# Edge softmax of a graph layer: 20 one-hot columns in four groups of five, 44 gathered columns, instead of 18 in three groups of six and 46 gathered

## The reference, cut to what matters

```
h = (x_flat @ W_gat).reshape(M, HEADS, NUM_EXPERTS)      # M = 16384 nodes, 4 x 4 values each
a_src = (h * att_src).sum(-1)
e = leaky_relu(a_src[src] + a_dst[dst], negative_slope=0.2)
e_max = segment_max(e, dst, num_segments=M)
ee = exp(e - e_max[dst])
denom = segment_sum(ee, dst, num_segments=M)
msg = h[src] * (ee / (denom[dst] + 1e-16))[:, :, None]
agg = segment_sum(msg, dst, num_segments=M)
```

## Time and profile before

| | |
|---|---|
| median of 3 runs | 7383.86 us (7380.45 to 7390.46) |
| the profiled execution | 7389.08 us, of which the span of its instructions is 7387.4 us |
| busy, share of the span | PE 76%, DVE 70%, ACT 37%, POOL 33% |
| the edge stage | from GpSimd's first gather at 3383.8 to about 5574 us |
| gathers in it (L2702) | 1472, busy 1718.7 us |
| matmuls of the columns (L2720) | 6912 |

### The profile page before, as it was taken

How to read it: one execution, slowest core, us unless ns; L and a number is a source line. 1 busy time by engine, 2 the same in 40 slices (tenths; PEclk the granted TensorE clock), 3 DMA queues, 4 the chain that set the end, 5 groups by cost and what they waited for, 6 DMA issues and landing times. The chain is left out here.

```text
span 7387.4 us, 113310 instructions
## 1 busy us (share of the span) xinstructions
PE 5582.5 (76%) x43709; PEld 2955.6 (40%) x43709; DVE 5138.4 (70%) x9355; ACT 2731.1 (37%) x4639; POOL 2413.2 (33%) x2214
## 2 busy tenths in 40 slices
PE   4759799868479999725978777877840579769998
PEld 3642266522146666522434333333420148623332
DVE  7869987877978888714866666666642466667776
ACT  3534433343256666512423223322310242323332
POOL 0000000000068400047777777777775210000000
PEclk8869899979779999957988889888975789879999
DMA  0000000012021000000111110110110000000001
GB/s 15 1 5 6 20 15 26 3 33 63 24 36 19 10 2 2 7 35 7 26 17 21 23 21 17 22 21 17 23 22 12 5 2 3 2 15 1 1 1 23
DMA packets 129314, 115.00 MB, mean 16 GB/s; under 512 B 72354, under 2 KB 113475, under 8 KB 127107
## 3 DMA queue, kind: packets, MB, share of 16 engines
q1 hardware_dynamic: 65278, 85.60, 3.9%
q0 software_dynamic: 63616, 23.35, 3.0%
q10 hardware_dynamic: 12, 0.39, 0.0%
HBM read 36.72 MB, written 37.86 MB: 10 GB/s over the span
## 5 line engine op out<-in xcount | busy, mean ns | idle before, releaser
L2702 POOL DMA_INDIRECT X<-gat_node_table,edges_idx x1472 | 1718.7, 1168 | 454.1 <-issue 454.1
L2720 PE MATMUL edges_bank<-XT,edges_hotT 128*128 128x512 bf16 x4608 | 1408.2, 388 | 0.0
L2720 PE MATMUL edges_bank<-X,edges_hotT 128*128 128x512 bf16 x2304 | 896.0, 389 | 388.3 <-ACT edges_hotT L2746 388.3
L2753 ACT COPY XT<-edges_bank 128x512 f32<-128x512 f32 x576 | 337.2, 585 | 993.1 <-PE edges_bank L2720 993.1
L2720 PEld LDWEIGHTS edges_bank<-XT,edges_hotT 128*128 128x128 bf16 x4608 | 459.1, 100 | 502.8 <-issue 47.4
L2720 PEld LDWEIGHTS edges_bank<-X,edges_hotT 128*128 128x128 bf16 x2304 | 229.7, 100 | 608.7 <-issue 413.7
L2821 DVE TENSOR_TENSOR XT<-XT,edges_mask 128x3072 f32<-128x3072 f32 x96 | 322.6, 3361 | 214.7 <-ACT XT L2753 169.8
L957 ACT ACTIVATE expd_act_out<-expd_hp 128x1024 f32<-128x1024 f32 x256 | 261.9, 1023 | 526.2 <-PE expd_hp L879 526.2
L989 DVE TENSOR_TENSOR expd_act_out<-expd_act_out,expd_h 128x1024 f32<-128x1024 f32 x256 | 312.7, 1221 | 201.6 <-ACT expd_act_out L957 201.5
L2746 ACT COPY edges_hotT<-edges_turn_p 128x512 bf16<-128x512 bf16 x576 | 340.4, 591 | 234.0 <-PE edges_turn_p L2712 233.8
L1399 ACT ACTIVATE GT<-attc_sc,attc_nm 128x256 f32<-128x256 f32 x1024 | 399.5, 480 | 36.5 <-DVE attc_nm L1465 36.5
(11 more groups left out here) (756 smaller groups left out, 11056.7 us busy)
## 6 DMA issues: line engine op xcount, KB each, us to landing
gat_states<-GT SPq DMA_DIRECT2D x32, 768.0 KB, 3.3
X<-gat_node_table,edges_idx POOLq DMA_INDIRECT x1472, 2.3
XT<-XT SPq DMA_DIRECT2D x32, 256.0 KB
XT<-XT SPq DMA_DIRECT2D x64, 128.0 KB
XT<-XT SPq DMA_DIRECT2D x128, 64.0 KB
gat_starts<-nodes_zeros SPq DMA_DIRECT2D x4, 1088.0 KB
attb_q<-attb_rows SPq DMA_DIRECT2D x256, 2.0 KB
XT<-XT SPq DMA_DIRECT2D x128, 32.0 KB
```

Source lines behind the costliest of these rows:

```text
L2702: nc.gpsimd.indirect_dma_start(out=rows[:, k, c, :], out_offset=None, in_=q.t_table, in_offset=bass.IndirectOffsetOnAxis(ap=idx[:, k, c:c ...
L2720: m = nc.tensor.matmul(banks[(k * ON_PE + t) % BANKS][:], hotT[:, t % 2, b * P:(b + 1) * P], parts[p][:, b].rearrange("p c u -> p (c u)"), ...
L2753: nc.scalar.copy(fetched[:, (k * GROUPS + t // PER_GROUP) % 2, t % PER_GROUP].rearrange("p c u -> p (c u)"), banks[(k * ON_PE + t) % BANKS ...
```

## The change

One line: the one-hot columns of a chunk become 4 groups of 5 (20 columns), the gathered ones 64 - 20 = 44, and the ring `fetched`, which has two groups, shrinks from 12 to 10 columns.

```
-    GROUPS, PER_GROUP = 3, 6
+    GROUPS, PER_GROUP = 4, 5
     ON_PE = GROUPS * PER_GROUP
     BY_DMA = C - ON_PE
```

## The result

The changed kernel takes **7338.82 us** (median of 4 runs, 7328.15 to 7349.08), the kernel before 7383.86: a ratio of 0.9936, interval 0.9923 to 0.9948, so 45 us less (38 to 57). The forecast was 7340, range 7307 to 7367.

A forecast was written before the change was run, and what follows sets the result against it. GpSimd's string of gathers was taken to set the stage's length. Fewer gathers (-74.9), product stalls (+22) and a later start (+9.5) summed to -43 us, giving 7340 us against the median, range 7307 to 7367.

The forecast's parts named there:

- The bound: GpSimd's string of gathers sets the stage's length, 1.248 us per gather plus stalls; a chunk costs 67.7 us.
- Two gathers fewer, -74.9: From the third chunk on, 60 fewer gathers at 1.248 us each save 74.9 us.
- Holds, +22: Gathers stalled by DVE's mask products L2821: 243 us in 30 chunks against 221, so +22 us.
- The comparisons L2811 hold nothing: DVE's one-hot comparisons stall no gather, as the gather of 4030.75 takes 0.94 us; the sum gives them none.
- the prediction's own sign of being wrong: DVE's gather wait going to nothing, L2821 stalls averaging over 2.3, or gathers stretched beside L2811 or L2823.
- The rival with the port locked by the comparisons: The comparisons L2811 hold gathers, 0.7 us more per chunk, 20 us in all, 7360; 3 in 100.
- The start, +9.5: The third block of gathers starts 9.5 us later, after eight products instead of six; nothing hides it.
- PE and DVE free: PE's two more columns (5.63 us per chunk) and DVE's +5 us fit in slack, 7 us left, costing nothing.
- The cover over TensorE: PE works 58.5 of some 66 us per chunk, so 7 us of its idle time stay.
- the dearer holds: Rival: a gather starts right with each product, each stall 2.71 us, +39 in sum, 7422; 4 in 100.
- a bound on TensorE: Rival: TensorE's 20 columns at the 1.2 GHz level take 93 us per chunk, 8140; 3 in 100.
- The cheaper holds: Rival: four products stall 1.85 us each, 7.4 per chunk; 7309 with the start hidden, otherwise 7318; 10 in 100.

The follow-up runs named there:

- the two experiments on the count of gathers: Kernel before with two gathers per chunk left out: 7307.48 us; changed kernel with two spare gathers per chunk added: 7407.02 us.
- the two PSUM edits: Changed kernel with the product's mask in PSUM: 7101.93 us; with the scans' decay factors in PSUM as well: 7050.61 us.
- that with six groups: Kernel before with its 18 one-hot columns in six groups of three: 7372.07 us.

## Why the prediction was right, point by point

- **The bound** (GpSimd's string): right, by the two experiments on the count of gathers, 74 and 68 us for 75.
- **Two gathers fewer, -74.9:** right.
- **Holds, +22:** measured +16, but made of other parts than forecast. The products were to bring +22 (243 us for 221). They brought +2: 219 us in 120 holds, 1.83 each instead of 2.02, against 217.5 in 90 before. The other +14 are the comparisons, +13, which the sum put at nothing, and the rest: scans 80 us for 83, small operations 13 for 9. By place in the chunk the four products hold 1.99, 1.70, 2.01 and 1.60 us, where the forecast had 2.0, 1.93, 2.08 and 2.08. The product lasts 2.83 as forecast. The second product comes 6.25 us after the first one's end in the chunk shown (4280.76 to 4287.01), not 6.71: five comparisons take 1.54 where six took 2.05, and the rest of `prepare` shortened too. So a gather starts together with it and goes free, and the next, 1.24 later, is held 1.48. The fourth was taken as drifting evenly, and isn't: in 27 of 30 chunks a gather starts within 0.04 us of it, goes free, and the next is held 1.48. The chunk shown, with 2.64 at the fourth, is one of the three others.
- **The comparisons L2811 hold nothing:** wrong, and the prediction's own sign of being wrong (gathers stretched beside L2811) came: 102 of the 120 groups hold a gather for 0.12 us, 13 us together. The row that the prediction took as proof couldn't decide it. At the point of the gather of 4030.75, 4030.87, the comparison that runs is 0.13 us old, too young to hold:

```profile
4030.74 0.34 DVE L2811 TENSOR_SCALAR GT<-edges_nodes,edges_place 128x512 bf16<-128x512 bf16 x1
```

The rival with the port locked by the comparisons, put at 3 in 100 and 20 us, thus came in its mechanism: a comparison does hold a gather to its own end. It came at 13 us, not by the two columns more but by the phase, from no such gather before to 102.

- **The start, +9.5:** 8.0. The eighth product started at 3514.66 for 3515.1; from there to L2848 it took 10.64 for 11.36, and from L2848 to the gather 7.09 for 7.35.
- **PE and DVE free:** right. DVE waits 7.8 for the forecast 7, PE pauses 6.6 for 7. The shorter pause doesn't spare PE the slow stretch behind it: after 5.33 us idle in the chunk shown, the granted clock is 0.50 (the 1.2 GHz level) from 4270.90 to 4276.00. The cover over TensorE is larger than I thought, since a TensorE that doesn't pause doesn't slow down.
- **Rivals:** neither the dearer holds nor a bound on TensorE came. The cheaper holds came in part: products at 1.83 each, the rival's 1.85, but with the start's +8 and the comparisons beside them. The kernel with the two gathers put back is the slower case of this change: 26 us, which is what the groups of five and the later start cost when nothing pays for them.

Sum of the terms as measured: -74.9 + 16 + 8.0 = -50.9, against -50.0 in the spans and -45 in the medians; the changed kernel's own runs spread over 21 us. The closeness of 7340 to 7338.82 is largely luck: the products' term was 20 us too dear and the comparisons' 13 too cheap, and they nearly cancel. With the measured product holds alone the forecast would have been 7320. The bound, the count of gathers and the start were right by their mechanism.

## What to carry to other kernels

When one engine issues without a pause and others wait for it once per round, count its instructions and look for those that are longer than the median: their ends, set beside another engine's, name what holds them. Here that list was worth 288 us (the two PSUM edits), six times the change itself, which only moved work away from the string. Small holds against a periodic string depend on the phase: work out the phase where the distance is fixed, and give bounds where it drifts. And a single undisturbed row doesn't show that an operation holds nothing: look first whether the row's phase was one at which it could be held.

## What the runs showed of the hardware

- An indirect gather issued by GpSimd is held by a VectorE tensor_tensor or scan whose two tensor inputs lie in SBUF, and ends 0.82 us after it; moving one input to PSUM removes the hold at no cost in VectorE time (2.82 us against 2.83; 20 scans 5.18 against 5.32). This agrees with the Trainium skill, "SBUF — State Buffer", "Reading the diagram", which names two SBUF inputs against a GpSimd operation that reads SBUF.
- The comparison L2811 has one tensor input (bf16, SBUF to SBUF) and holds a gather too, to its own end: 102 gathers in the changed kernel, 172 in that with six groups, 0.12 to 0.13 us each. The sum L2823, as long as the product, holds none: 240 gathers of the changed kernel have their point in one. The same page of the Trainium skill, in its box on VectorE blocking DMA, has operations in a two-port mode keep GpSimd from writing descriptors; the comparisons fit that, but no run shows in which mode they ran. The large cost here came from two-input operations: 300 of the 309 us of holds in the kernel before (217.5 by products, 83 by scans).
- Of the gathers that start within the 20 scans of the chunk shown (4272.41 to 4277.73), that of 4273.50 takes 1.13 us, and only that of 4274.94 is held to the scans' end. Why the earlier one passes stays open.
- A gather that gets to its point (0.12 us after its start) while the operation is younger than 0.16 us goes free: beside 46 of the 120 products of the changed kernel one starts within 0.04 us of the product and takes no longer than 0.95.
- TensorE's granted clock was 1.00 throughout the stretch without pauses (3700 to 5000, mask in PSUM), and 0.94 in the changed kernel with pauses of 6.6 us (0.88 before, with 13.9).
